# Three half-size weight buffers, squares on ScalarE, and projection weights staged in the arena of a three-part transformer layer

## The chip, the cores and the metric

The kernel runs on 8 cores of one Trainium2 chip. Each core takes 2 of the 16 sequences and works alone: no core talks to another. The metric is the device time in microseconds (us) of the slowest core.

TensorE (PE) multiplies, VectorE (DVE) and ScalarE (ACT) do the elementwise work and empty PSUM, GpSimd (POOL) and SyncE (SP) only issue DMA transfers here. ACT issues DMA transfers as well, from its own queue of instructions.

## The reference, cut to what matters

```python
def layernorm(x): return (x - mean(x)) / sqrt(var(x) + 1e-5)

def ffn(x):                       # D = 1024, H = 4096, per sequence of 2048
    h = x @ W1.T + scale * (x @ m1.T) + b1      # m1, m2: rank-4 products of
    h = gelu(h)                                 # rows 1..16 of x itself
    return h @ W2.T + scale * (h @ m2.T) + b2

def attn(x):                      # 8 heads of 128, causal
    xn = x / l2norm(x) * sqrt(1024) * gamma
    q, k, v = split(xn @ w_qkv.T)
    return softmax(mask(q @ k.T * 128**-0.5)) @ v @ w_out.T

x = x + 0.5 * ffn(layernorm(x))
x = x + attn(layernorm(x))
x = x + 0.5 * ffn(layernorm(x))
```

## The kernel before, in words

Everything is kept transposed: features on the 128 partitions, tokens along the free dimension. `R` holds the residual of one sequence in f32 (8 feature chunks `cc` of 2048 tokens), `xn` its normalised bf16 copy, and `arena` (64 KB in each partition, tracked as 32 slots of 1024 columns) holds either the hidden layer of an FFN tile of 1024 tokens or, in attention, four regions of 8192 columns: K at `KT0` (slots 0 to 7), V at `V0` (8 to 15), Q at `QT0` (16 to 23) and the attention output at `OA0` (24 to 31), for 4 heads at a time.

The program is one list of operations, written by Python in the order of the source. Each goes to the queue of one engine and keeps its place there; the class `Buf` works out from writers and readers of each slot which semaphores it waits for. So an instruction that waits holds up all behind it on its engine, DMA issues on SP and ACT among them. DMAs of one `group` also wait for the one before them in the group.

At the start `emit_prep` turns the f32 weights into bf16 in DRAM (`w1s`, `w2s`, `wqs`, `wos`) by way of arena slots 0 to 15. Then, for each of the 2 sequences: FFN, attention, FFN.

- **FFN** (`ffn`): 2 token tiles `ti` of 1024. The first product (L728, with the rank-4 part L739 and the GELU on ACT, L746) runs over 32 hidden chunks `hc`. Weights come by `wslab("w1", g, ...)`: 512 KB with 2 chunks, in turn into `wb0` and `wb1`. For each `nh` (512 tokens), 32 small matmuls (L765) and their evictions (L774) come first, then the second product (L797) over all hidden chunks into 8 PSUM banks at once; `wslab("w2", g, ...)` brings 2 chunks a time. Bias (ACT, L818) and residual (DVE, L826) end it, and then a *hook* runs.
- **LayerNorm** (`ln_block`, 512 tokens): sums over features by matmul with a column of ones (L473), squares on DVE (L483) into two halves of `sqt`, their sums by matmul (L488), then a chain of short row operations on ACT and DVE (L498 to L528), two rows sent to DRAM and back as broadcasts `rep_a` and `rep_b` (four DMAs issued by ACT, one group), and 16 DVE operations that write `xn` (L546/L550, or L553/L558 with gamma). In the first FFN the hook of `ti` 0, `nh` 0 has two such blocks in a row and that of `ti` 1, `nh` 0 has three, that of `ti` 1, `nh` 1 one. In attention, `attn_hook` puts one after each of the four token blocks of the last output projection; the one at `qb` 2 comes behind `lora_prep(part=1)`, with eight DMAs `e1z<-t` on ACT.
- **Attention** (`attn`), for each half `hh` of the heads: Q, K, then V projections from xn. `wslab` brings each weight as two slabs of 512 KB, part 0 to `wb0` and part 1 to `wb1`; every accumulation reads both. Q and K are evicted by ACT (L930, L926), V by DVE (L958), from 2 PSUM banks. After each head of K, `mhat_head` works out a bound for the softmax: 8 rounds of DVE square (L854), PE sum (L860), DVE maximum (L866), then Sqrt on ACT, and one number through DRAM (`browN`, `negm`), issued by ACT. Then units of 512 queries of a head: scores (L975, L986), Exp on ACT (L996), row sums (L1009) and P·V (L1019), and last the output projection (L1094, residual L1107) with two slabs of `wos`.

The two-buffer rotation:

```python
def next_w():
    i = wrot[0] % 2
    wrot[0] += 1
    return (wb0, "wb0") if i == 0 else (wb1, "wb1")
```

Of the kernel before, what the change touches and what calls it, by code (L numbers as in the profile page):

```python
# [251 lines left out]
def build(n_sub=3):  # L252
# [28 lines left out]
    with ctx:  # L281
# [146 lines left out]
        def wslab(kind, arg, wt, wbname, part=0):  # L428
            if kind == "w1":
                gate = prep_done["w1"][arg // 4]  # L430
            elif kind == "w2":
                gate = prep_done["w2"][arg // 4]
            elif kind in ("wq", "wk", "wv"):
                gate = prep_done["wq"][2 * part + 1]
            else:
                gate = prep_done["wo"][arg]
            deps = B(wbname).deps_write() + [gate]
            if kind == "w1":
                src = w1s[:, arg * 256:(arg + 1) * 256].rearrange("(cc p) h -> p cc h", p=128)
                dst = wt[:, :].rearrange("p (cc h) -> p cc h", cc=CC)  # L440
            elif kind == "w2":
                src = w2s[arg * 256:(arg + 1) * 256, :].rearrange("(hh p) o -> p hh o", p=128)
                dst = wt[:, :].rearrange("p (hh o) -> p hh o", hh=2)
            elif kind in ("wq", "wk", "wv"):
                f0 = {"wq": 0, "wk": 1, "wv": 2}[kind] * DM + arg * 512
                src = wqs[part * 512:(part + 1) * 512, f0:f0 + 512].rearrange(
                    "(cc p) f -> p cc f", p=128)
                dst = wt[:, :].rearrange("p (cc f) -> p cc f", cc=4)
            elif kind == "wo":
                r0 = arg * 512 + part * 256  # L450
                src = wos[r0:r0 + 256, :].rearrange("(fc p) c -> p fc c", p=128)
                dst = wt[:, :].rearrange("p (fc c) -> p fc c", fc=2)
# [794 lines left out]
```

How the kernel before makes its waits and increments, by code:

```python
            def run(engine_obj):  # L128
                hiwater = {}
                for op in oplist:
                    waits = {}
                    for d, m in op.deps:
                        if elided(e, d):
                            continue
                        s, v = d.sem, d.val
                        if m:
                            mo = margin_tok(d, op)
                            if mo is not None and mo.dma_group is None:
                                s, v = mo.tok.sem, mo.tok.val
                        assert s is not None, (e, op.tag, d.eng, d.idx)
                        if hiwater.get(s, 0) >= v:
                            continue
                        if waits.get(s, 0) < v:
                            waits[s] = v
                    for s, v in waits.items():
                        engine_obj.wait_ge(get_sem(s), v)
                        hiwater[s] = v
                        stats["waits"] += 1
                    ins = op.fn(engine_obj)
                    if op.needs_inc:
                        amt = 16 if op.dma_group is not None else 1
                        ins.then_inc(get_sem(op.tok.sem), amt)
                        stats["incs"] += 1
```

## Time and profile before

| | us |
|---|---|
| median of the 2 timed runs | 5114.68 (4993.43 and 5235.94) |
| the profiled execution, own time | 5005.92 |
| its span on the slowest core (core 1) | 5003.9 |
| spans of the 8 cores | 4958.5 to 5003.9 |
| PE busy | 3785.2 (76%) |
| ACT busy | 1165.2 (23%) |
| DVE busy | 868.2 (17%) |
| DMA traffic | 335.24 MB, mean 67 GB/s |

The span runs from the first to the last instruction; 2.0 us of the time lie around it. PE is busy for three quarters of the span, and what it waits for in the rest decides what a change is worth. A busy matmul of 128x512 is listed with a mean of 385 ns, but successive ones overlap: in a dense stretch one starts every 0.22 us. The granted clock of TensorE was 0.873 of full speed over the span of this core.

### The profile page before, as it was taken

To read this page: it belongs to the slowest core of one execution; us is meant where nothing else is said; L and a number is where in the kernel's file an instruction comes from. 1 tells how busy PE (TensorE), PEld (TensorE's weight loads), DVE (VectorE), ACT (ScalarE), POOL (GpSimd) and SP (SyncE) were. 2 spreads that over 40 slices of the span, in tenths; PEclk is the share of its full clock that TensorE was granted. 3 is DMA by queue.
4 is the path that set the end of the run, shared out by engine and by line. 5 is a ranking of instruction groups with operands and counts; after the bars stand their busy time and mean duration, and the time that the engine had idled before them with its cause. 6 is when DMAs were issued, how large, how long until landed. Compare 5 with 4: busy or idle time off the path is not lost.

```text
span 5003.9 us, 42288 instructions; the slowest of 8 cores (4958.5 to 5003.9 us)
## 1 busy us (share of the span) xinstructions
PE 3785.2 (76%) x14576; PEld 1307.5 (26%) x14576; DVE 868.2 (17%) x1403; ACT 1165.2 (23%) x1819; POOL 63.7 (1%) x114
## 2 busy tenths in 40 slices
PE   2068699676886865978969869957688686597997
PEld 0023133122222211323323313312222221133333
DVE  2000300523023034001010030052302303400000
ACT  0012121111631621311212212111163162131211
POOL 0000000000000000000000000000000000000000
PEclk7579799788997987989989979978799798798997
DMA  9952122120000000234233213212000000023323
GB/s 193 204 126 68 51 89 88 47 63 19 24 26 19 22 15 26 59 102 126 69 105 118 68 51 89 89 47 63 19 22 28 19 22 15 26 59 102 102 86 112
DMA packets 275837, 335.24 MB, mean 67 GB/s; under 512 B 20080, under 2 KB 163824, under 8 KB 275632
## 3 DMA queue, kind: packets, MB, share of 16 engines
q1 hardware_dynamic: 232688, 251.98, 16.6%
q0 software_dynamic: 18144, 50.34, 5.0%
q10 hardware_dynamic: 24800, 30.23, 2.1%
q8 instruction: 124, 2.03, 0.2%
q14 instruction: 81, 0.66, 0.0%
HBM read 315.16 MB, written 42.47 MB: 71 GB/s over the span
## 4 chain that ended last, share of the span: by engine, by line
PE 59%; DMA 20%; DVE 8%; ACT 6%; issue 6%; ACTq 1%; DVEq 0%; another core or an unknown queue 0%; SPq 0%; POOL 0%; POOLq 0%
PE ps L728 19%; PE ps L797 12%; DMA wb<-w2s 7%; PE ps L911 5%; PE ps L739 3%; PE ps L1009 3%; PE ps L1019 3%; PE ps L944 2%; PE ps L1094 2%; PE ps L765 2%; PE ps L986 2%; PE ps L473 2%; DMA arena<-w2T 2%; DMA rep_a<-browL 1%; ACT pb L996 1%
## 5 line engine op out<-in xcount | busy, mean ns | idle before, releaser
L728 PE MATMUL ps<-xn,wb 128*128 128x512 bf16 x4096 | 987.7, 385 | 105.6 <-DMA wb<-w1s 89.8
L797 PE MATMUL ps<-arena,wb 128*128 128x512 bf16 x4096 | 931.3, 385 | 66.9 <-DMA wb<-w2s 62.0
L797 PEld LDWEIGHTS ps<-arena,wb 128*128 128x128 bf16 x4096 | 392.7, 99 | 604.5 <-issue 212.3
L728 PEld LDWEIGHTS ps<-xn,wb 128*128 128x128 bf16 x4096 | 361.6, 98 | 598.1 <-issue 242.3
L746 ACT ACTIVATE arena<-ps,b1c 128x512 bf16<-128x512 f32 x512 | 351.3, 687 | 715.0 <-PE ps L739 698.8
L826 DVE SCALAR_TENSOR_TENSOR R<-f32t,R 128x512 f32<-128x512 f32 x128 | 88.6, 692 | 2462.8 <-ACT f32t L818 2462.8
L996 ACT ACTIVATE pb<-ps,negm 128x512 bf16<-128x512 f32 x640 | 419.3, 686 | 231.8 <-PE ps L986 135.1
L818 ACT ACTIVATE f32t<-ps,b2c 128x512 f32<-128x512 f32 x128 | 88.0, 687 | 1088.1 <-PE ps L811 987.9
L911 PE MATMUL ps<-xn,wb 128*128 128x512 bf16 x1024 | 273.3, 431 | 53.6 <-DMA wb<-wqs 22.3
L1009 PE MATMUL ps<-pb,onesc 128*1 128x512 bf16 x640 | 247.6, 387 | 80.3 <-ACT pb L996 80.3
L1019 PE MATMUL ps<-pb,arena 128*128 128x512 bf16 x640 | 255.6, 399 | 11.8 <-DVE arena L1047 11.8
L488 PE MATMUL ps<-sqt,onesc 128*1 128x512 bf16 x192 | 92.0, 494 | 227.0 <-DVE sqt L483 225.9
L986 PE MATMUL ps<-arena 128*128 128x512 bf16 x640 | 244.4, 391 | 17.7 <-ACT pb L996 17.7
L1094 PE MATMUL ps<-arena,wb 128*128 128x512 bf16 x512 | 137.5, 433 | 158.8 <-DVE R L1107 131.3
L473 PE MATMUL ps<-R,onesf 128*1 128x512 f32 x384 | 189.2, 646 | 46.7 <-DMA R<-xT 34.6
L739 PE MATMUL ps<-t,e1z 4*128 4x512 bf16 x512 | 198.6, 388 | 0.0
L860 PE MATMUL ps<-sqt,onesc 128*1 128x512 bf16 x128 | 65.5, 511 | 151.0 <-DVE sqt L854 151.0
L1047 DVE TENSOR_TENSOR arena<-ps,f32t 128x512 bf16<-128x512 f32 x64 | 44.2, 691 | 714.0 <-DMA f32t<-browF 305.9
L691 PE MATMUL ps<-xn,o1c 128*4 128x512 bf16 x160 | 63.7, 549 | 136.6 <-ACT t L700 58.6
L911 PEld LDWEIGHTS ps<-xn,wb 128*128 128x128 bf16 x1024 | 108.0, 108 | 218.2 <-issue 131.1
L866 DVE TENSOR_REDUCE nrm<-ps 1x1 f32<-1x512 f32 x128 | 86.9, 679 | 324.0 <-PE ps L860 324.0
L483 DVE TENSOR_TENSOR sqt<-R 128x512 bf16<-128x512 f32 x192 | 124.2, 687 | 106.3 <-PE ps L488 103.3
(81 smaller groups left out, 1810.2 us busy)
## 6 DMA issues: line engine op xcount, KB each, us to landing
wb<-w2s SPq DMA_DIRECT2D x256, 512.0 KB, 3.5
wb<-w1s SPq DMA_DIRECT2D x128, 512.0 KB, 4.0
f32t<-browF ACTq DMA_DIRECT2D x64, 256.0 KB
outT<-R POOLq DMA_DIRECT2D x64, 256.0 KB, 3.5
wb<-wqs SPq DMA_DIRECT2D x24, 512.0 KB, 4.0
arena<-w1T POOLq DMA_DIRECT2D x4, 2048.0 KB, 30.2
w1s<-arena SPq DMA_DIRECT2D x4, 2048.0 KB, 13.9
arena<-w2T POOLq DMA_DIRECT2D x4, 2048.0 KB, 39.0
```

Of the source, the lines that this page charges most:

```text
L473: t_sa = p.emit("pe", lambda e, cc=cc, n0=n0: e.matmul(ps[6][0:1, :], onesf[:, :], rsl(cc, n0), start=(cc == 0), stop=(cc == CC - 1)), dep ...
L483: t_sq = p.emit("dve", lambda e, cc=cc, n0=n0, pr=pr: e.tensor_mul(sqt[:, pr * 512:(pr + 1) * 512], rsl(cc, n0), rsl(cc, n0)), deps=B("R") ...
L728: t_mm = p.emit("pe", lambda e, cc=cc, hcl=hcl, n0=n0, wt=wt, bank=bank: e.matmul(bank[:, :], wt[:, cc * 256 + hcl * 128: cc * 256 + (hcl ...
L739: t_c1 = p.emit("pe", lambda e, hc=hc, nh=nh, bank=bank: e.matmul(bank[:, :], e1z[:, hc * 128:(hc + 1) * 128], t1[:, nh * 512:(nh + 1) * 5 ...
L746: t_g = p.emit("act", lambda e, hc=hc, nh=nh, bank=bank: e.activation(h_act(hc, nh), bank[:, :], AF.Gelu, bias=b1c[:, hc:hc + 1]), deps=[t ...
L797: t_mm = p.emit("pe", lambda e, oc=oc, hcl=hcl, hc=hc, nh=nh, wt=wt, bank=bank: e.matmul(bank[:, :], wt[:, hcl * 1024 + oc * 128: hcl * 10 ...
L911: t_mm = p.emit("pe", lambda e, cc=cc, ccl=ccl, h=h, nb=nb, wt=wt, bank=bank: e.matmul(bank[:, :], wt[:, ccl * 512 + h * 128: ccl * 512 + ...
L986: t_s = p.emit("pe", lambda e, kcol=kcol, qcol=qcol, bank=bank, diag=diag: e.matmul(bank[:, :], arena[:, kcol:kcol + 128], arena[:, qcol:q ...
L996: t_e = p.emit("act", lambda e, pslot=pslot, h=h, bank=bank: e.activation(pb[:, pslot * 512:(pslot + 1) * 512], bank[:, :], AF.Exp, bias=n ...
L1009: t_rs = p.emit("pe", lambda e, pslot=pslot, first=first, last=last, rsb=rsb: e.matmul(rsb[0:1, :], onesc[:, :], pb[:, pslot * 512:(pslot ...
L1019: t_pv = p.emit("pe", lambda e, vcol=vcol, pslot=pslot, first=first, last=last, ob=ob: e.matmul(ob[:, :], arena[:, vcol:vcol + 128], pb[:, ...
L1094: t_mm = p.emit("pe", lambda e, fc=fc, fcl=fcl, oc=oc, ocol=ocol, wt=wt, bank=bank: e.matmul(bank[:, :], wt[:, fcl * 1024 + oc * 128: fcl ...
```

## The change

1. Weight buffers: `wb0`, `wb1` of 2048 columns become `wb0`, `wb1`, `wb2` of 1024, in rotation. A slab holds one hidden chunk, 256 KB. So there are 32 slabs where there were 16. A `w1` slab was 1024 runs of 512 B (256 columns of 8 rows for each partition); now it is 1024 runs of 256 B. A `w2` slab was 256 runs of 2 KB and is 128.
2. `ln_block`: the squares are made by `activation(Square)` on ACT in place of `tensor_mul` on DVE.
3. Attention: V is projected first, then Q, then K. Each weight comes as one DMA of 1 MB into the arena: V's into the first half of the Q region, Q's and K's into the output region; the output projection's into the first half of the K region. `wb` isn't used there.

```diff
-        wb0 = sb("wb0", [128, 2048], BF16)
-        wb1 = sb("wb1", [128, 2048], BF16)
+        wb0 = sb("wb0", [128, 1024], BF16)
+        wb1 = sb("wb1", [128, 1024], BF16)
+        wb2 = sb("wb2", [128, 1024], BF16)
...
             if kind == "w1":
-                src = w1s[:, arg * 256:(arg + 1) * 256].rearrange("(cc p) h -> p cc h", p=128)
+                src = w1s[:, arg * 128:(arg + 1) * 128].rearrange("(cc p) h -> p cc h", p=128)
...
         def next_w():
-            i = wrot[0] % 2
+            i = wrot[0] % 3
             wrot[0] += 1
...
-                    t_sq = p.emit("dve", lambda e, cc=cc, n0=n0, pr=pr: e.tensor_mul(
-                        sqt[:, pr * 512:(pr + 1) * 512], rsl(cc, n0), rsl(cc, n0)),
+                    t_sq = p.emit("act", lambda e, cc=cc, n0=n0, pr=pr: e.activation(
+                        sqt[:, pr * 512:(pr + 1) * 512], rsl(cc, n0), AF.Square),
...
-                for g in range(16):
+                for g in range(32):
                     wt, wbn = next_w()
                     t_w = wslab("w1", g, wt, wbn)
...
-                for kind, reg0, scale_ev in (("wq", QT0, SCALE_ATTN), ("wk", KT0, None), ("wv", V0, None)):
-                    t_w0 = wslab(kind, hh, wb0, "wb0", part=0)
-                    t_w1 = wslab(kind, hh, wb1, "wb1", part=1)
...
+                def qkv_slab(kind, hh, col0):
+                    gate = prep_done["wq"][1]
+                    f0 = {"wq": 0, "wk": 1, "wv": 2}[kind] * DM + hh * 512
+                    src = wqs[:, f0:f0 + 512].rearrange("(cc p) f -> p cc f", p=128)
+                    dst = arena[:, col0:col0 + 4096].rearrange("p (cc f) -> p cc f", cc=CC)
+                    sl = aslot(col0, 4096)
+                    t = p.dma("sp", dst, src, deps=B("arena").deps_write(sl) + [gate],
+                              group="wA", tag=f"{kind}{hh}")
...
+                t_wv, wv_sl = qkv_slab("wv", hh, QT0)
+                for tt in range(16):
...
+                t_wq, wq_sl = qkv_slab("wq", hh, OA0)
+                t_wk, wk_sl = qkv_slab("wk", hh, OA0 + 4096)
...
-                t_wo0 = wslab("wo", hh, wb0, "wb0", part=0)
-                t_wo1 = wslab("wo", hh, wb1, "wb1", part=1)
+                src = wos[hh * 512:(hh + 1) * 512, :].rearrange("(fc p) c -> p fc c", p=128)
+                wo_sl = aslot(KT0, 4096)
+                dst = arena[:, KT0:KT0 + 4096].rearrange("p (fc c) -> p fc c", fc=4)
```

The first place where this moves instructions is DVE between two gamma-fused LayerNorm blocks of the first FFN's second tile. Before, the last write of `xn` of one block is followed by the next block's squares:

```order
L553 SCALAR_TENSOR_TENSOR f32t<-R,gamc,rep_a 128x512
L558 SCALAR_TENSOR_TENSOR xn<-rep_b,gamc,f32t 128x512
L483 TENSOR_TENSOR sqt<-R 128x512 x8
L506 TENSOR_TENSOR srow_c<-srow_a 1x512
L510 TENSOR_TENSOR srow_b<-srow_b,srow_c 1x512
L515 TENSOR_SCALAR srow_b<-srow_b 1x512
```

Now ACT has the squares, behind the two broadcast issues of the block before and ahead of its own short rows (L496 and L500 are L498 and L502 of before):

```order
L70 DMA rep_a<-browL 128x512
L70 DMA rep_b<-browL 128x512
L481 ACTIVATE sqt<-R 128x512 x8
L496 ACTIVATE srow_a<-ps 1x512
L500 ACTIVATE srow_b<-ps 1x512
L516 ACTIVATE srow_b<-srow_b 1x512
```

On DVE the block's first short row (L504, before L506) therefore stands right behind the last write of `xn`; on PE this place is unchanged.

The second place is PE from the last LayerNorm block of the first FFN to the first scores. Before, Q and the first head of K (160 matmuls), three more heads of K, then V, and the scores:

```order
L488 MATMUL ps<-sqt,onesc 1x512 x8
L911 MATMUL ps<-xn,wb 128x512 x160
L860 MATMUL ps<-sqt,onesc 1x512 x8
...
L911 MATMUL ps<-xn,wb 128x512 x32
L860 MATMUL ps<-sqt,onesc 1x512 x8
L944 MATMUL ps<-wb,xn 128x512 x128
L975 MATMUL ps<-maskm,ident 128x512
```

Now V comes first, and the bound of the last head is followed at once by the scores:

```order
L486 MATMUL ps<-sqt,onesc 1x512 x8
L913 MATMUL ps<-arena,xn 128x512 x128
L943 MATMUL ps<-xn,arena 128x512 x160
L858 MATMUL ps<-sqt,onesc 1x512 x8
...
L943 MATMUL ps<-xn,arena 128x512 x32
L858 MATMUL ps<-sqt,onesc 1x512 x8
L981 MATMUL ps<-maskm,ident 128x512
L992 MATMUL ps<-arena 128x512
```

V's 128 matmuls moved from between the last bound and the scores to the front, where the block of LayerNorm before them is still being written by DVE.

## Rows read from the trace of the kernel before

**Rows 1.** Groups by line (busy us, mean ns; idle before and its releasers).

```profile
L728 PE MATMUL ps<-xn,wb 128*128 128x512 bf16 x4096 | 987.7, 385 | 105.6 <-DMA wb<-w1s 89.8 <-ACT f32t L818 10.5 <-ACT arena L746 5.3
L797 PE MATMUL ps<-arena,wb 128*128 128x512 bf16 x4096 | 931.3, 385 | 66.9 <-DMA wb<-w2s 62.0 <-ACT u L774 3.1
...
L911 PE MATMUL ps<-xn,wb 128*128 128x512 bf16 x1024 | 273.3, 431 | 53.6 <-DMA wb<-wqs 22.3 <-DVE xn L558 16.1 <-ACT arena L930 12.6
...
L488 PE MATMUL ps<-sqt,onesc 128*1 128x512 bf16 x192 | 92.0, 494 | 227.0 <-DVE sqt L483 225.9
...
L518 ACT ACT_TABLE_LOAD x6 | 7.7, 1283 | 8.7 <-DVE srow_b L515 8.7
```

**Rows 2.** Waits: who waited for whom, us in total, times, longest us.

```profile
PE ps L797 <- DMA wb<-w2s: 62.0, 107, 2.5
```

**Rows 3.** Timeline of a second product: start us, us, engine, line, what, [idle before].

```profile
2155.42 7.08 PE L797 MATMUL ps<-arena,wb 128*128 128x512 bf16 x32
...
2159.13 3.81 SPq L70 DMA_DIRECT2D wb<-w2s  x2
...
2163.24 1.02 PE L797 MATMUL ps<-arena,wb 128*128 128x512 bf16 x4 [0.73 <-DMA wb<-w2s]
```

**Rows 4.** Windows: stretch, PE, PEld, DVE, ACT, POOL busy, PEclk, DMA share, GB/s.

```profile
470.00:520.00 50.00, 47.70 (x215) 20.12 (x214) 0.00 (x0) 0.00 (x0) 0.00 (x0) 1.00 0.42 137
690.00:810.00 120.00, 120.00 (x504) 44.12 (x503) 0.00 (x0) 38.31 (x57) 0.00 (x0) 1.00 0.21 62
```

**Rows 5.** DMA queue issued by ACT: packets, MB, share of 16 engines.

```profile
q10 hardware_dynamic: 24800, 30.23, 2.1%
```

**Rows 6.** Timeline of ACT's queue, the two broadcasts of a LayerNorm block.

```profile
1833.33 0.35 ACTq L70 DMA_DIRECT2D rep_a<-browL  x1
1836.42 0.35 ACTq L70 DMA_DIRECT2D rep_b<-browL  x1
```

**Rows 7.** Timeline of the hook with three LayerNorm blocks, first sequence.

```profile
917.34 0.35 ACTq L70 DMA_DIRECT2D rep_b<-browL  x1
...
932.58 0.75 DVE L558 SCALAR_TENSOR_TENSOR xn<-rep_b,gamc,f32t 128x512 bf16<-128x512 f32 x1
933.25 1.28 DVE L483 TENSOR_TENSOR sqt<-R 128x512 bf16<-128x512 f32 x2
...
940.82 0.68 DVE L510 TENSOR_TENSOR srow_b<-srow_b,srow_c 1x512 f32<-1x512 f32 x1 [0.99 <-ACT srow_b L502]
...
972.81 0.68 DVE L510 TENSOR_TENSOR srow_b<-srow_b,srow_c 1x512 f32<-1x512 f32 x1 [0.99 <-ACT srow_b L502]
...
982.57 7.93 PE L797 MATMUL ps<-arena,wb 128*128 128x512 bf16 x28 [2.13 <-ACT u L774]
```

**Rows 8.** Timeline of PE at the switch from Q to K.

```profile
1117.20 8.35 PE L911 MATMUL ps<-xn,wb 128*128 128x512 bf16 x32 [3.05 <-DMA wb<-wqs]
```

**Rows 9.** Timeline of the start of attention, PE and DVE.

```profile
1064.62 3.63 PE L911 MATMUL ps<-xn,wb 128*128 128x512 bf16 x16
...
1089.38 0.75 DVE L558 SCALAR_TENSOR_TENSOR xn<-rep_b,gamc,f32t 128x512 bf16<-128x512 f32 x1
...
1090.27 23.88 PE L911 MATMUL ps<-xn,wb 128*128 128x512 bf16 x97 [1.12 <-DVE xn L558]
```

**Rows 10.** Timeline from the last softmax bound of a half to its first exponentials.

```profile
1205.83 29.14 PE L944 MATMUL ps<-wb,xn 128*128 128x512 bf16 x128
...
1209.56 0.33 ACTq L70 DMA_DIRECT2D negm<-browN  x1
...
1235.48 1.28 ACT L996 ACT_TABLE_LOAD   x1 [27.48 <-PE ps L986]
...
1237.61 0.38 PE L1009 MATMUL ps<-pb,onesc 128*1 128x512 bf16 x1 [0.60 <-ACT pb L996]
```

**Rows 11.** Timeline of ACT in the attention hook at qb 2.

```profile
1920.65 5.64 ACTq L70 DMA_DIRECT2D e1z<-t  x4
...
1927.97 0.59 ACT L502 ACTIVATE srow_b<-ps 1x512 f32<-1x512 f32 x1 [0.99 <-PE ps L488]
```

More of the change, by code:

```diff
@@ L433, in wslab @@
+                dst = wt[:, :].rearrange("p (hh o) -> p hh o", hh=1)
             elif kind in ("wq", "wk", "wv"):
-                gate = prep_done["wq"][2 * part + 1]
+                gate = prep_done["wq"][part // 2]
+                f0 = {"wq": 0, "wk": 1, "wv": 2}[kind] * DM + arg * 512
+                src = wqs[part * 256:(part + 1) * 256, f0:f0 + 512].rearrange(
+                    "(cc p) f -> p cc f", p=128)
+                dst = wt[:, :].rearrange("p (cc f) -> p cc f", cc=2)
             else:
@@ L436, in wslab @@
                 gate = prep_done["wo"][arg]
+                r0 = arg * 512 + part * 128
+                src = wos[r0:r0 + 128, :].rearrange("(fc p) c -> p fc c", p=128)
+                dst = wt[:, :].rearrange("p (fc c) -> p fc c", fc=1)
             deps = B(wbname).deps_write() + [gate]
-            if kind == "w1":
-                src = w1s[:, arg * 256:(arg + 1) * 256].rearrange("(cc p) h -> p cc h", p=128)
[L440 to L452, printed above, removed]
@@ L788, in ffn @@
                     B("u4").wrote(t_uin)
-                    for g in range(16):
+                    for g in range(32):
                         wt, wbn = next_w()
@@ L793, in ffn @@
                             bank, bn = ps[oc], f"ps{oc}"
[L794 to L798 removed]
+                            for hcl in range(1):
+                                hc = g
+                                first = (hc == 0)
+                                t_mm = p.emit("pe", lambda e, oc=oc, hc=hc, nh=nh, wt=wt, bank=bank: e.matmul(
+                                    bank[:, :], wt[:, oc * 128:(oc + 1) * 128],
                                     h_act(hc, nh), start=(hc == 0), stop=False),
@@ new lines, in attn @@
+                t_wv, wv_sl = qkv_slab("wv", hh, QT0)
+                for tt in range(16):
+                    bank, bn = ps[tt % 2], f"ps{tt % 2}"
+                    last = None
+                    for cc in range(CC):
+                        t_mm = p.emit("pe", lambda e, cc=cc, tt=tt, bank=bank: e.matmul(
+                            bank[:, :], xn[:, cc * S + tt * 128: cc * S + (tt + 1) * 128],
+                            arena[:, QT0 + cc * 512: QT0 + (cc + 1) * 512],
+                            start=(cc == 0), stop=(cc == CC - 1)),
+                            deps=[t_wv] + B("xn").deps_read(rslot(cc, tt * 128)) +
+                                 (B(bn).deps_write() if cc == 0 else []), tag="wvmm")
+                        B("arena").read(t_mm, wv_sl)
+                        B("xn").read(t_mm, rslot(cc, tt * 128))
+                        if cc == 0:
+                            B(bn).wrote(t_mm)
+                        else:
+                            B(bn).accum(t_mm)
+                        last = t_mm
+                    col0 = V0 + tt * 512
+                    slots = aslot(col0, 512)
+                    t_ev = p.emit("dve", lambda e, col0=col0, bank=bank: e.tensor_copy(
+                        arena[:, col0:col0 + 512], bank[:, :]),
+                        deps=[last] + B("arena").deps_write(slots), tag="wvev")
+                    B(bn).read(t_ev)
+                    B("arena").wrote(t_ev, slots)
@@ L940, in attn @@
+                t_wq, wq_sl = qkv_slab("wq", hh, OA0)
+                t_wk, wk_sl = qkv_slab("wk", hh, OA0 + 4096)
+                for kind, wcol, wtok, wsl, reg0, scale_ev in (
+                        ("wq", OA0, t_wq, wq_sl, QT0, SCALE_ATTN),
+                        ("wk", OA0 + 4096, t_wk, wk_sl, KT0, None)):
+                    for h in range(HPH):
+                        for nb in range(4):
+                            bank, bn = ps[nb % 2], f"ps{nb % 2}"
                             last = None
@@ L951, in attn @@
+                                B("arena").read(t_mm, wsl)
+                                B("xn").read(t_mm, rslot(cc, nb * 512))
                                 if cc == 0:
```

106 lines of the change are left out of this document (36 added, 70 removed).

## The prediction

> **What bounds the kernel now.** I read the groups by line first, to see on what PE waits. PE is busy 3785.2 of 5003.9 us, so 1219 us are idle, and neither DVE nor ACT is busy for a quarter of it. The groups show three idle times that the change touches [rows 1]: 62.0 us before the second product L797, released by `wb<-w2s`; 22.3 us before the Q and K products L911, released by `wb<-wqs`; and 225.9 us before the sums of squares L488, released by the DVE squares. They show too where there is nothing to win: L728 waits on its weights once, 89.8 us at the start, behind the conversion of the weights, which the change leaves alone.
>
> Next the waits: the 62.0 us are 107 waits, none over 2.5 [rows 2], so a small shortfall that repeats. The timeline shows why [rows 3]. PE does 32 matmuls, two slabs, in 7.08 us; the slab issued at 2159.13, when the first buffer came free, releases PE at 2163.24, 4.11 us later, while the other buffer lasts about 3.6. So each pair of slabs costs some 0.5 to 0.7 us.
>
> Last, the timelines of the hooks. In them the chain is DVE's: it writes xn of one LayerNorm block until 933.3, only then squares the next one, and the variance row comes at 940.82 [rows 7].
>
> **The second product.** Three buffers of half the size leave the same cover: a buffer is refilled during two slabs of 8 matmuls, which is again 3.6 us. What changes is how long a slab takes. A w2 slab is now 128 rows of 2 KB, which is what the broadcast `rep_a` moves; issued at 1833.33 it had landed by 1836.42, 3.09 us later [rows 6]. With the 0.1 us in which SP sees the buffer free this is 3.2, less than 3.6: the wait goes. I keep 8 of the 62.0 us for stragglers and take -54. Bounds: -62, and if a half slab took the 4.11 us of a whole one, (4.11 - 3.63) x 512 slabs / 3 = 82 in place of 62, so +20. The row of the same shape is the nearest, so I stay near the lower end.
>
> **The first product.** The runs shrink from 512 to 256 B, and their number stays, 1024 for each slab, so it doubles in all. What a run costs now: in the window 690 to 810, 62 GB/s x 120 us are 14,500 runs of 512 B, and 0.21 x 16 engines x 120 us = 403 us, 27.7 ns each [rows 4]. The same from the window 470 to 520 gives 100 ns for 2 KB. Runs below 512 B are in ACT's queue: of its 24,800 packets 14,336 are rows of 2 KB (64 + 48 broadcasts of 128); at 100 ns they take 1439 of its 2.1% x 16 x 5003.9 = 1681 us and leave 23 ns for each of the 10,464 small ones [rows 5]. So a run of 256 B lies between 23 and 28 ns, at most 68, the mean over that queue. At 28 a slab keeps an engine busy for 64 x 28 ns = 1.8 us, and PE needs 18 matmuls x 120 us / 504 = 4.29 us for it [rows 4]. I take 0. The cover that would have to go is 4.29 us for 64 runs, 67 ns each.
>
> The Trainium skill speaks against this edit ("DMA: Bandwidth & Descriptors", Specifications): transfers reach line rate only from 512 B up, below that the engine reads, modifies and writes. No price is given there; if it meant twice the time of a 512 B run, 55 ns, the slab would take 3.5 us and would still be hidden, at a DMA share of 0.8. The trace shows no sign of it in the small packets of ACT's queue, but no row has runs of exactly this size.
>
> **Projection weights.** Q, K and V weights now go to regions that are free long before they are read: V's slots (16 to 19) during the last second product or after head 1's scores, Q's and K's during V. The wait of 22.3 us goes [rows 1]. There are three such switches in a sequence (Q to K twice, output projection to Q once). After one of them 32 matmuls took 8.35 us [rows 8] against 7.08 in a dense stretch [rows 3], so PE started slowly; 1.3 us x 6 are 8 us more. I take -30, bounds -22 and -32. The output weights were never waited for, so the fourth DMA is worth 0.
>
> **LayerNorm blocks that follow one another.** ACT issues `rep_b` of block 1 at 917.34 and is then free; its eight squares, 0.7 to 0.77 us each with PE's sums between, would be done by 924, well before DVE ends block 1 at 933.3 [rows 7]. DVE then goes straight to the short rows, and the variance row stands at 933.3 + 0.6 = 933.9 in place of 940.82: 6.9 us sooner. So again for the third block. It is this chain that ends the stall, not the squares alone: PE gets past block 3's sums much sooner, does its 32 small matmuls, and then waits for ACT to empty them, which is queued behind block 3's own broadcasts. That point, 982.57, moves by the chain's 2 x 6.9 and not by the 22 us by which PE's wait on squares shrinks. The hook of `ti` 0 has one such pair. Three pairs in each of two sequences: 6 x 6.9 = -41. The first block of each hook starts its squares half a DVE operation sooner, 8 blocks x 0.5 = -4. In attention's last projection the residual of the next block waits for DVE's writes of xn, and the squares wait for that residual on either engine: 0. Sum -45, bounds -41 (pairs only) and -60 (were the third block's earlier start all gain).
>
> ACT holds the squares at 0.69 us as its other 128x512 operations, and no table is loaded for them, which is my choice: a load takes 1.283 us, and 24 blocks would add 31 us at one each, 62 at two [rows 1]. The Trainium skill says that cheap functions are in every table set ("ScalarE: Activation LUTs", Table sets: the hidden batching unit), though its list doesn't name Square; by that rule the term is 0. The trace of before has no Square at all.
>
> **What the change adds.** (a) V is evicted by DVE, and V now comes first. In each sequence's first half DVE is writing xn until 1089.38 + 0.75 = 1090.1 [rows 9], so PE stops after two banks, 16 matmuls, near 1068 and goes on at 1090.8 with 112 + 128 to do. Before, at 1090.27, it had 97 + 128 left: 15 x 0.22 + 0.6 = +4 us, twice, +8. (b) The last head's bound was hidden by V. Its PE part ends at 1205.9, and ACT is free when `negm` is issued, 1209.56 + 0.33; behind that wait the table load 1.28 and the first Exp 0.69, 1211.9, so PE is without work for 6.0 us; before, the same point lay 2.7 us after V's end (1234.9 to 1237.61) [rows 10]. +3.3 x 4 = +13, bounds 0 and +24. (c) At `qb` 2 the squares stand on ACT behind eight DMAs `e1z<-t`, which last until 1926.3; the second sum came in at 1927.97 [rows 11]. Now eight squares of 0.61 to 0.69 come between, +5 x 2 = +10, bounds 0 and +12.
>
> **The sum.** -54 - 30 - 45 + 8 + 13 + 10 = -98. Against the profiled execution's own time, 5005.92 (its span and 2.0 around it), 4908 us. The median of the two runs shown, 5114.68, lies 109 above that execution, since one of the two took 5235.94; the other, 4993.43, agrees with it. The forecast is for executions like those two. It is 2.0% below, and 2% is about what a measurement of this kernel can tell, so this lies on the line.
>
> **The rivals.**
> - *The half slab takes nearly as long as the whole.* The waits of the second product stay at about 62 to 82. For it: 512 KB of w2 land in 4.11 us and 512 B runs of the same volume no slower, so much of a transfer is fixed. Against: 3.09 for the same shape [rows 6]. Time: 4908 + 54 to 74, about 4975. Chance 0.15.
> - *First product becomes DMA-bound: slower than before.* Place: every slab of L728, 256 of them. It decides from 67 ns for a run of 256 B, and outweighs the gains from 64 x p - 4.29 = 98 / 256 = 0.38 us on, p = 73 ns. At 80 ns: 0.83 x 256 = 212, 5120 us. For it: the halved runs, 8 cores at once. Against: 23 to 28 ns, and even the queue's mean of 68 is at the edge only. Chance 0.09.
> - *Table loads for Square.* +31 to +62 where half of them lie on the chain: about 4940 to 4970. Chance 0.08.
> - *More is gained than the waits.* PE restarts slowly after each of the long stalls in the hooks and projections, as in rows 8; if shorter stalls save this too, some 24 times 1.3 us, 4877. For it: mean granted clock 0.873. Against: the stalls of the hooks stay over 10 us. Chance 0.18.
> - *The change doesn't do what it says,* the chain behind DVE and ACT absorbing LayerNorm's part (-45 gone): 4953. Chance 0.08.
>
> The forecast has the remaining 0.42. Faster by over 2% (below 4906): half of the forecast's own 0.42 and most of the gain rival's 0.18 and a few of the others' tails, 0.43. Slower by over 2%: the DMA-bound case from 80 ns on, 0.06. Within 2%: 0.51. The range takes in all but the DMA-bound case and the far ends of the others; on the high side it adds the mishap of two small losses together: 4840 to 5030.
>
> **What would show it.** In the profile after: `PE ps L797`'s successor with under 15 us of waits on w2s and a landing below 3.6; no wait on w1s but the one at the start, and a DMA share near 0.4 in its windows, twice the 0.21 of before because the packets double (0.8 if a small run costs twice as much, 1.0 if the rival holds); no wqs waits; variance rows 26 us apart in the three-block hook where they were 32; PE idle for 6 us after each half's last bound, and for 22 after the first 16 V matmuls; table loads still near 22 in all. Wrong would be: w1s waits in numbers, or w2s waits as many as before.

## The result and the profile after

| | before | after |
|---|---|---|
| median of all timed runs | 4998.61 us (10 runs) | 4895.52 us (11 runs) |
| median of the 7 that count on each side | 4993.43 us | 4894.10 us |
| ratio, with its 95% interval | | 0.9798 [0.9786, 0.9809] |
| the profiled execution, own time | 5005.92 us | 4899.44 us |
| spans of the 8 cores | 4958.5 to 5003.9 us | 4865.5 to 4897.9 us |
| mean span of the 8 cores | 4983.9 us | 4878.8 us |

The change makes the kernel 2.0% faster, on the line between "same" and "faster" as forecast. In some executions four of the cores, or all eight, ran at a lower clock and took longer; the ratios and every median from here on leave them out (e8 has no other), and a trace that was taken in one (e1, e6, e8) is read only as far as is said there.

The groups by line of the kernel after, on its slowest core, beside [rows 1]:

```profile
L726 PE MATMUL ps<-xn,wb 128*128 128x512 bf16 x4096 | 986.8, 384 | 124.5 <-DMA wb<-w1s 108.4 <-ACT f32t L816 10.8 <-ACT arena L744 5.3
L795 PE MATMUL ps<-arena,wb 128*128 128x512 bf16 x4096 | 894.4, 380 | 32.2 <-ACT u L772 22.0 <-DMA wb<-w2s 9.6
L943 PE MATMUL ps<-xn,arena 128*128 128x512 bf16 x1024 | 246.3, 405 | 2.3 <-ACT arena L958 2.3
L913 PE MATMUL ps<-arena,xn 128*128 128x512 bf16 x512 | 116.7, 391 | 46.5 <-DVE arena L928 46.5
L486 PE MATMUL ps<-sqt,onesc 128*1 128x512 bf16 x192 | 93.8, 509 | 125.1 <-ACT sqt L481 118.0
L481 ACT ACTIVATE sqt<-R 128x512 bf16<-128x512 f32 x192 | 112.3, 623 | 228.2 <-PE ps L486 89.3 <-DVE R L1115 62.3 <-DMA rep_a<-browL 61.1
L516 ACT ACT_TABLE_LOAD x6 | 7.7, 1283 | 8.7 <-DVE srow_b L513 8.7
```

Four things are to be seen. The second product, now L795, waits 9.6 us for `w2s` where it waited 62.0, but also 22.0 us for ACT's `u`, and its *busy* time fell too, 931.3 to 894.4 on the slowest cores. The first product has one wait on `w1s`, as before:

```profile
PE ps L726 <- DMA wb<-w1s: 108.4, 1, 108.4
PE ps L795 <- ACT u L772: 22.0, 2, 11.0
PE ps L795 <- DMA wb<-w2s: 9.6, 13, 1.6
```

That one is the start (first product at 298.4 us before and 300.5 after, mean of the cores). The projections wait on no weights; V waits 46.5 us on its DVE evictions. And the sums of squares wait 118.0 us where they waited 225.9: 108 us of idle time less, in a kernel that became 105 us faster by all its edits together. Table loads are 22 in both, the group of six unchanged.

To see where the time went I cut each core's PE timeline at the same points in both kernels and took the mean over the 8 cores:

| stretch | before | after | difference | forecast |
|---|---|---|---|---|
| 16 second products | 984.0 | 925.4 | -58.6 | |
| hooks of the FFNs with LayerNorm | | | -66.2 | |
| the same two, ACT's wait for `u` (3.4 to 22.4) moved from the first to the second | | | -77.6; -47.2 | -54; -45 |
| projections Q, K, V, 4 halves | 649.3 | 623.3 | -26.0 | |
| output projection to the next half's Q or V | | | -7.5 | with the line above -22 |
| scores to the last P·V, 4 halves | 724.6 | 768.5 | +43.9 | +13 |
| attention hooks, 2 | 381.9 | 393.6 | +11.7 | +10 |
| start | 298.4 | 300.5 | +2.1 | 0 |
| 8 first products | 1127.1 | 1122.4 | -4.7 | 0 |
| whole | 4983.9 | 4878.8 | -105 | -98 |

The rows add up to -105, as the whole does. The 4.7 us of the first products are no gain of the change: they lie in the very first tile, which took 146.4 us in this execution of the kernel before, 139.5 in the kernel after, and 139.6 in e2 and e3 with the slabs of before.

So the total hides errors that nearly cancel: 24 us more gained in the buffers and 11.5 more in the projections than forecast, and 31 more lost in the scores. The scores are the surprise: they were not edited. This is the first half on one and the same core, a window from the first score to the last P·V (columns as in [rows 4]), before and then after:

```profile
1235.00:1416.00 181.00, 152.96 (x543) 38.28 (x541) 11.06 (x16) 122.78 (x191) 0.00 (x0) 0.98 0.09 28
```

```profile
1195.00:1392.00 197.00, 165.38 (x545) 39.28 (x544) 11.63 (x20) 123.30 (x193) 0.00 (x0) 0.91 0.11 31
```

The same instructions, the same 123 us of ACT; the column PEclk falls from 0.98 to 0.91 and the window is 16 us longer. Over the four halves, mean of the cores, the granted clock was 0.99, 0.964, 0.99, 0.984 before and 0.923, 0.945, 0.926, 0.944 after, that is less time at the upper of its two levels, 2.4 GHz. The halves don't lose alike: the two first ones went from 179.4 to 194.4 us, the two second ones from 184.6 and 181.1 to 189.8 and 189.7. On core 1 the second half of the first sequence didn't change at all, 188 us at 0.95 before and after:

```profile
1610.00:1798.00 188.00, 159.62 (x546) 38.75 (x544) 11.06 (x16) 122.78 (x191) 0.00 (x0) 0.95 0.09 27
```

```profile
1572.00:1760.00 188.00, 156.89 (x544) 38.83 (x543) 11.63 (x20) 123.11 (x192) 0.00 (x0) 0.95 0.12 32
```

Nor is it an even slowdown. The first 15 us of each half of the kernel after, and the rest (same core, first half and then second half):

```profile
1195.00:1210.00 15.00, 10.32 (x27) 2.31 (x26) 1.26 (x5) 7.14 (x12) 0.00 (x0) 0.78 0.01 1
1210.00:1392.00 182.00, 155.05 (x518) 36.98 (x518) 10.37 (x15) 116.16 (x183) 0.00 (x0) 0.92 0.12 34
1572.00:1587.00 15.00, 10.93 (x27) 2.32 (x26) 1.26 (x5) 6.50 (x10) 0.00 (x0) 0.60 0.01 1
1587.00:1760.00 173.00, 145.97 (x517) 36.50 (x517) 10.37 (x15) 116.61 (x182) 0.00 (x0) 0.98 0.13 34
```

PE enters both halves partly at the lower level. In the first half it also falls back to it again and again later (0.92 over the rest; 8 of the 13 windows of 15 us in it show 0.89), in the second hardly (0.98).

### The profile page after: what moved, and what is told of

Read it like the earlier page. It is cut to its first block, busy times and chain, and to the rows that moved or that the text cites. A ratio compares the mean times of both kernels' runs of the same rounds, so it can differ in the third digit from the quotient of the medians.

```text
span 4897.9 us, 43897 instructions; the slowest of 8 cores (4865.5 to 4897.9 us)
## 1 busy us (share of the span) xinstructions
PE 3756.5 (77%) x14576; PEld 1311.6 (27%) x14576; DVE 747.6 (15%) x1211; ACT 1275.4 (26%) x2011; POOL 63.7 (1%) x114
## 4 chain that ended last, share of the span: by engine, by line
PE 65%; DMA 14%; DVE 7%; ACT 7%; issue 5%; ACTq 1%; DVEq 0%; another core or an unknown queue 0%; SPq 0%; POOL 0%; POOLq 0%
PE ps L726 19%; PE ps L795 17%; PE ps L943 5%; PE ps L737 3%; PE ps L1015 3%; PE ps L1025 3%; PE ps L1102 2%; PE ps L763 2%; PE ps L913 2%; PE ps L992 2%; DMA browF<-srow_a 2%; DMA arena<-w2T 2%; DMA rep_a<-browL 1%; ACT pb L1002 1%; ACT f32t L816 1%
## 5 line engine op out<-in xcount | busy, mean ns | idle before, releaser
L726 PE MATMUL ps<-xn,wb 128*128 128x512 bf16 x4096 | 986.8, 384 | 124.5 <-DMA wb<-w1s 108.4
L795 PE MATMUL ps<-arena,wb 128*128 128x512 bf16 x4096 | 894.4, 380 | 32.2 <-ACT u L772 22.0
L795 PEld LDWEIGHTS ps<-arena,wb 128*128 128x128 bf16 x4096 | 397.8, 98 | 527.9 <-issue 60.3
L726 PEld LDWEIGHTS ps<-xn,wb 128*128 128x128 bf16 x4096 | 361.4, 98 | 615.8 <-issue 259.5
L992 PE MATMUL ps<-arena 128*128 128x512 bf16 x640 | 255.1, 408 | 19.7 <-ACT pb L1002 19.7
L1102 PE MATMUL ps<-arena 128*128 128x512 bf16 x512 | 143.7, 448 | 155.2 <-DVE R L1115 127.5
L943 PE MATMUL ps<-xn,arena 128*128 128x512 bf16 x1024 | 246.3, 405 | 2.3 <-ACT arena L958 2.3
L486 PE MATMUL ps<-sqt,onesc 128*1 128x512 bf16 x192 | 93.8, 509 | 125.1 <-ACT sqt L481 118.0
L481 ACT ACTIVATE sqt<-R 128x512 bf16<-128x512 f32 x192 | 112.3, 623 | 228.2 <-PE ps L486 89.3
L913 PE MATMUL ps<-arena,xn 128*128 128x512 bf16 x512 | 116.7, 391 | 46.5 <-DVE arena L928 46.5
L1015 PEld LDWEIGHTS ps<-pb,onesc 128*1 128x1 bf16 x640 | 50.6, 79 | 374.5 <-issue 374.5
```

The costliest lines, as they stand in the source:

```text
L726: t_mm = p.emit("pe", lambda e, cc=cc, n0=n0, wt=wt, bank=bank: e.matmul(bank[:, :], wt[:, cc * 128:(cc + 1) * 128], xsl(cc, n0), start=(c ...
L795: t_mm = p.emit("pe", lambda e, oc=oc, hc=hc, nh=nh, wt=wt, bank=bank: e.matmul(bank[:, :], wt[:, oc * 128:(oc + 1) * 128], h_act(hc, nh), ...
L913: t_mm = p.emit("pe", lambda e, cc=cc, tt=tt, bank=bank: e.matmul(bank[:, :], xn[:, cc * S + tt * 128: cc * S + (tt + 1) * 128], arena[:, ...
L943: t_mm = p.emit("pe", lambda e, cc=cc, h=h, nb=nb, wcol=wcol, bank=bank: e.matmul(bank[:, :], arena[:, wcol + cc * 512 + h * 128: wcol + c ...
L992: t_s = p.emit("pe", lambda e, kcol=kcol, qcol=qcol, bank=bank, diag=diag: e.matmul(bank[:, :], arena[:, kcol:kcol + 128], arena[:, qcol:q ...
L1015: t_rs = p.emit("pe", lambda e, pslot=pslot, first=first, last=last, rsb=rsb: e.matmul(rsb[0:1, :], onesc[:, :], pb[:, pslot * 512:(pslot ...
```

## The experiments

Ten kernels ran, e1 to e10. The kernel before ran beside each of them, the kernel after did not; differences to the kernel after are taken from its 4894.10 us, those to the kernel before from its 4993.43.

### One part at a time: which edit gives what

e1 is the kernel after with its squares back on DVE, so buffers and attention alone:

```diff
-                    t_sq = p.emit("act", lambda e, cc=cc, n0=n0, pr=pr: e.activation(
-                        sqt[:, pr * 512:(pr + 1) * 512], rsl(cc, n0), AF.Square),
+                    t_sq = p.emit("dve", lambda e, cc=cc, n0=n0, pr=pr: e.tensor_mul(
+                        sqt[:, pr * 512:(pr + 1) * 512], rsl(cc, n0), rsl(cc, n0)),
```

> The changed kernel with the squares back on DVE, so attention part plus three half-size buffers. Beside the kernel with the attention part alone it gives the price of the buffers. Theory A (a stall costs more than the idle time listed for it, because the last matmul before it runs out its full 380 ns in place of the 216 ns pitch): the buffers are worth about 95 us, the sum of the 16 second products falls from 998 to about 900 us. Rival B (my forecast: only the listed 62 us can go): about 54 us. Time: A 4905, B 4945. Without the squares on ACT there is no ACT-bound wait of 12 us at the start of two of the second products.

Measured 4920.98 us (4920.15 and 4921.80), ratio 0.9839 [0.9697, 0.9981]. Of its trace only the waits are read, on core 1:

```profile
PE ps L795 <- DMA wb<-w2s: 8.5, 11, 3.0
PE ps L795 <- ACT u L772: 4.4, 2, 2.7
```

The waits on `w2s` are down to 8.5 us without the squares too, and of the 22 us of waits on ACT only 4.4 are there: the rest belongs to the squares.

e2 is the kernel before with only that edit made (Square on ACT).

> The kernel before with the squares on ACT alone. Chain theory: three pairs of blocks in each of two sequences save 6.9 us each (-41), singles -4, the block behind the e1z DMAs loses 5 to 6 in each sequence (+10 to +12): -33, about 4965. Rival (the squares on ACT only move the wait): no change, 4998. Variance rows in the three-block hook 26 us apart in place of 32, table loads still 22 to 23.

Measured 4960.13 us in the one execution that counts, 33 below the kernel before, as the chain theory said; one execution gives no interval. Its hooks agree with those of the kernel after to 0.2 us (first sequence, mean of the cores: the two-block hook 77.6 before and 70.2 and 70.0 now; the three-block hook 84.8 and 61.0 in both), and so do its attention hooks (196.9 and 197.0, before 191.1 and 190.8). The squares' part is thus separate from the rest: -47.2 in the FFNs and +11.7 in attention, -35.5.

e3 is the kernel before with only part 3 of the change, attention's order and weights.

> The kernel before with the attention part alone (V, Q, K order, weights staged in the arena, V's evictions on DVE, two full-size buffers elsewhere). Theory A (the order V, Q, K takes away a dense run ahead of the scores, and their granted clock falls from 1.00 to about 0.91): projections gain about 35 us, the scores lose about 30, so about 4995, and the scores of a first half take 193 to 197 us where they took 181. Rival B (my forecast: -30, +8, +13 from waits alone): the scores lose 3.3 us each, about 4989, at a clock of 1.00.

Measured 5004.15 us, ratio 1.0017 [0.9977, 1.0057]. The attention part alone gives nothing. It saves the same on the projections (first halves 171.7 to 167.8, second 153.3 to 142.9) and loses it in the scores: 767.2 against 724.6, granted clock 0.934, 0.925, 0.963, 0.921. Theory A is near by its total (4995) and its sizes (-35 and +30 expected; -36, the switch to the next half with it, and +42 measured), though not by the place: the first halves took 191.5 and 188.2 us, under the 193 to 197 expected, and the second ones 193.4 and 193.9, more than in the kernel after. Its second product waits as before:

```profile
PE ps L797 <- DMA wb<-w2s: 68.7, 116, 2.8
```

From e3 to e1 is the buffers alone: 5004.2 to 4921.0, -83 (-79 between the fastest executions), which agrees with the -77.6 of the table and not with the -54 of the forecast, nor with the 95 that theory A gave.

**Where the other 24 us of the buffers were.** e2 and the kernel after have the same squares and the same waits on ACT, so their second products differ by the buffers alone: 999.3 and 925.4, 74 us. The listed waits on `w2s` fell by 51.3 (59.8 to 8.5, mean of the cores), as forecast; the busy time of L797 fell by 21.6 (914.6 to 893.0). A matmul followed closely by another counts its pitch, 216 ns (the 7.08 us of 32 in [rows 3] are 31 x 0.216 and one of 0.38), and the last before a stall counts its whole 0.38. Each of the 101 stalls that went (114 to 13, mean of the cores) therefore also took 0.16 us of "busy" with it, 16 us (an estimate); stalls shorter than that wouldn't be listed at all, which may be the other 5, but that is argued and not measured.

### The order of Q, K and V: why the scores became slower

e4 is the kernel after with Q, K and V in the old order and the weights still in the arena (Q's and K's in V's region, V's in the output region):

```diff
-                t_wv, wv_sl = qkv_slab("wv", hh, QT0)
-                for tt in range(16):
...
+                t_wq, wq_sl = qkv_slab("wq", hh, V0)
+                t_wk, wk_sl = qkv_slab("wk", hh, V0 + 4096)
+                do_qk("wq", V0, t_wq, wq_sl, QT0, SCALE_ATTN)
+                t_wv, wv_sl = qkv_slab("wv", hh, OA0)
+                do_qk("wk", V0 + 4096, t_wk, wk_sl, KT0, None)
+                do_v(range(16), OA0, t_wv, wv_sl, "dve")
```

> The changed kernel with the order Q, K, V again, all weights still staged in the arena (Q's and K's in the V region, V's in the output region). It takes away V's stall behind DVE and puts the dense V run back ahead of the scores. Clock theory: the scores of a first half take 181 to 183 us again at a granted clock of 1.00 for most of it (193 to 197 at about 0.91 in the changed kernel), and all four scores together give back about 30 us, the V stall another 8: 38 us below the changed kernel, 4858. Rival (only the uncovered tail of the last bound, 3.3 us four times, and the stall): 21 us, 4875, with the clock of the scores unchanged.

Median 4882.0 us, lowest 4870.75, ratio 0.973 [0.9644, 0.9816]: 12 below the kernel after by the medians, 21.5 by the mean span of the profiled executions. The scores are back to 737.5 from 768.5; in the first half core 1 is again at 0.98 and 181 us:

```profile
1197.00:1378.00 181.00, 153.37 (x545) 38.45 (x543) 11.07 (x16) 122.95 (x191) 0.00 (x0) 0.98 0.11 34
```

The projections cost 622.6, as in the kernel after (623.3): the weights in the arena are what gains, and the new order is what costs. V first puts the stop-and-go products of the last bound straight ahead of the scores; V last puts 128 dense matmuls there. So the order explains 31 of the 43.9 us that the scores lost, the uncovered hole of 3.3 us four times among them. The other 13 are there with V last too (737.5 against 724.6); most of that is in the second halves (187.6 and 187.3), and it stays open. The time misses the 4858 of the clock theory by 24: by those 13, and because the 8 us of V's stall didn't come. The first halves' projections gained 2.4 us each, the second ones lost 1.4 and 2.5, and the switch from output projection to the next half went from 37.1 to 40.4, twice.

e6 splits V in the first half: tiles 0 to 11 first, evicted by ACT, then Q and K, then tiles 12 to 15, so that 32 dense matmuls stand ahead of the scores; the second half goes Q, K, V.

```diff
+                    do_v(range(12), OA0 + 4096, t_wv, wv_sl, "act")
+                    do_qk("wq", KT0, t_wq, wq_sl, QT0, SCALE_ATTN)
+                    do_qk("wk", OA0, t_wk, wk_sl, KT0, None)
+                    do_v(range(12, 16), OA0 + 4096, t_wv, wv_sl, "dve")
```

> As e4, but in the first half of each sequence V's first 12 token tiles come first, with evictions on ACT, and its last 4 after K. It should keep what e4 gains on the tail of the bound and what e5 gained at the start: if both causes are real and separate, 4830 to 4845, the fastest of all. If 32 dense matmuls (7 us) ahead of the scores are too few for the clock, the scores of the first half stay near 190 us and the time lies near 4850.

Median 4855.29 us, lowest 4849.61, ratio 0.9676 [0.957, 0.9781]; the stages are read from e9 below, which has the same order. That is 39 below the kernel after, but short of the 4830 to 4845 expected and near the 4850 of the case in which 32 dense matmuls are too few.

### V's evictions

e5 is the kernel after with V evicted by ACT in each sequence's first half, where DVE is still writing xn:

```diff
+                    if hh == 0:
+                        t_ev = p.emit("act", lambda e, col0=col0, bank=bank: e.copy(
+                            arena[:, col0:col0 + 512], bank[:, :]),
```

> The changed kernel with V's evictions on ACT in the first half of each sequence. If the 23 us stall behind V's first two banks is DVE writing xn, PE goes on as soon as ACT has issued the second broadcast, about 16 us sooner, twice: -32, about 4863. Rival (V would wait for xn of the last token block anyway): V reaches that block only after 96 matmuls, 21 us, so at most 3 us of the gain are lost; if it waited sooner the gain would be under 10 us in all.

Median 4864.17 us, ratio 0.9726 [0.9645, 0.9807]; -30, and -32 was expected. The stall it removes, in the kernel after on core 3, and what is left of it in e5 on core 1:

```profile
1030.09 3.63 PE L913 MATMUL ps<-arena,xn 128*128 128x512 bf16 x16
...
1055.41 0.75 DVE L556 SCALAR_TENSOR_TENSOR xn<-rep_b,gamc,f32t 128x512 bf16<-128x512 f32 x1 [0.17 <-DVE f32t L551]
1056.91 18.28 PE L913 MATMUL ps<-arena,xn 128*128 128x512 bf16 x73 [23.20 <-DVE arena L928]
```

```profile
1022.54 3.63 PE L913 MATMUL ps<-arena,xn 128*128 128x512 bf16 x16
1033.32 0.13 PEld L913 LDWEIGHTS ps<-arena,xn 128*128 128x128 bf16 x2 [7.65 <-issue]
1033.35 16.96 PE L913 MATMUL ps<-arena,xn 128*128 128x512 bf16 x71 [7.18 <-ACT arena L929]
```

PE stops after 16 matmuls in both, for 23.2 and for 7.2 us; the first half's projections go from 168.5 to 152.2. The scores gain nothing (773.7 against 768.5), so a shorter stall at the head of the projections doesn't bring their clock back.

### The hook at qb 2

e7 is the kernel after with `ln_block` ahead of `lora_prep`, so that the squares stand before the eight DMAs `e1z<-t` on ACT:

```diff
                     elif qb == 2:
-                        lora_prep(part=1)
                         ln_block(NT, False)
+                        lora_prep(part=1)
```

> The changed kernel with ln_block(NT) ahead of lora_prep(part=1) in the attention hook at qb 2, so the squares on ACT don't stand behind the e1z DMAs. Theory: the 5 to 6 us by which the attention hooks grew in each sequence come back and some of lora_prep hides behind the LayerNorm chain: -12 to -30, about 4875. Rival (lora_prep's own PE and ACT steps now wait behind the broadcasts instead): 0, 4896.

Measured 4862.2 us (4857.27 to 4866.94), ratio 0.9696 [0.959, 0.9801]; -32, beyond the expected range by 2. The hooks take 181.2 each in place of 196.8. In the kernel after, ACT's timeline shows the squares behind the DMAs, and PE then waits 20.77 us for the residual that DVE does after its xn writes:

```profile
1889.63 5.62 ACTq L70 DMA_DIRECT2D e1z<-t  x4
...
1895.35 1.15 ACT L481 ACTIVATE sqt<-R 128x512 bf16<-128x512 f32 x2 [5.80 <-DMA e1z<-t]
...
1901.68 0.59 ACT L500 ACTIVATE srow_b<-ps 1x512 f32<-1x512 f32 x1 [0.35 <-PE ps L486]
...
1926.66 5.65 PE L1102 MATMUL ps<-arena 128*128 128x512 bf16 x13 [20.77 <-DVE R L1115]
```

In e7 the second sum leaves ACT at 1881.02, the DMAs follow behind the broadcasts, and PE restarts without that wait:

```profile
1881.02 0.59 ACT L500 ACTIVATE srow_b<-ps 1x512 f32<-1x512 f32 x1 [0.35 <-PE ps L486]
...
1898.87 5.62 ACTq L70 DMA_DIRECT2D e1z<-t  x4
...
1899.45 3.59 PE L1102 MATMUL ps<-arena 128*128 128x512 bf16 x8
...
1906.40 5.95 PE L1102 MATMUL ps<-arena 128*128 128x512 bf16 x19 [3.36 <-ACT t L620]
```

### How far w1 is from being bound by its transfers

e8 loads each w1 slab twice into the same buffer, doubling the small runs and nothing else:

```diff
+            if kind == "w1":
+                t = p.dma("sp", dst, src, deps=deps, group=grp, tag=f"{kind}{arg}.x")
+                B(wbname).wrote(t)
+                deps = B(wbname).deps_write() + [gate]
```

> The changed kernel with every w1 slab loaded twice, one after the other, before it is used. Runs of 256 B cost 18 ns in the changed kernel's window (0.28 x 16 x 110 us over 27,000 runs): two loads in series take about 2 x 3.0 us from issue, 6.1, under the 8.6 us of cover, so no wait on w1s beyond the start and a DMA share near 0.56; time within 10 us of the changed kernel. Rival (small runs near their limit with 8 cores at once): waits on w1s in numbers, over 100 us more.

It has no time that counts (4998, 5010 and 5127 us). The stage can be read on core 0, whose granted clock (0.874) is that of the kernel after. The window of the first product, in the kernel after (core 3) and in e8 (core 0):

```profile
680.00:790.00 110.00, 110.00 (x462) 40.52 (x461) 0.00 (x0) 36.15 (x53) 0.00 (x0) 1.00 0.28 63
```

```profile
690.00:790.00 100.00, 98.43 (x407) 36.39 (x415) 0.00 (x0) 31.62 (x46) 0.00 (x0) 1.00 0.56 120
```

In the kernel after 63 GB/s x 110 us are 27,070 runs of 256 B, and 0.28 x 16 x 110 = 493 us, 18.2 ns each, less than the 27.7 of a 512 B run [rows 4] though not half of it. In e8 the share doubles to 0.56 and PE is nearly always busy; its waits on w1s go from one to 30,

```profile
PE ps L730 <- DMA wb<-w1s: 128.4, 30, 105.8
```

of which 105.8 is the start, so 22.6 us are new, 0.09 for each of 256 slabs. As in the second product the stage lost more than is listed: the eight first products of core 0 took 1152.2 us against 1123.1, 29 us, which alone is more than the 10 expected for the whole kernel (mean of all cores +45, not all at that clock). The whole span of core 0 is only 10.5 longer, 4896.9 against 4886.4, since its scores took 23 less. Twice the runs are mostly hidden, not wholly; at the single load the cover is far from gone.

### The best version

e9 joins e6's order and e7's swap; e10 joins e4's order and e7's swap. No edit is new.

> The split V order and the swapped hook together. If the two gains add (scores and projections in one, 15.7 us in each of two attention hooks in the other), about 31 below the split order alone, 4815 to 4825, ratio near 0.962. If 32 dense matmuls ahead of the scores are enough for the clock, the scores of a first half take 180 to 183 us at 0.98; if not, near 190.

> The order Q, K, V with staged weights and the swapped hook. Gains add: 31 below the order Q, K, V alone (4871), 4840, ratio near 0.966; scores 737 us in all as in that kernel, attention hooks 181 each.

e9: median 4816.12 us (4806.95 to 4820.68), ratio 0.9623 [0.9596, 0.9649], 1.6% below the kernel after: the best. The gains add: against the kernel after the projections take 30 us less, the scores 33, the attention hooks 31, and the switch to the next half 6 more. Its scores are 183.3, 183.0, 184.8, 184.0, sum 735.1; in the first half of core 1:

```profile
1175.00:1359.00 184.00, 155.87 (x542) 38.42 (x541) 11.02 (x16) 122.46 (x191) 0.00 (x0) 0.96 0.12 34
```

With 32 dense matmuls ahead of the scores the first halves run at 0.973 and 0.960 (mean of the cores), between the 0.923 and 0.926 of none in the kernel after and the 0.985 and 0.977 of 128 in e4. The mean hides a scatter: in the second sequence three cores took 192 us at 0.92, as without any, and three 177.5 to 177.7 at 1.00. And the second halves of e9, where Q, K and V are those of e4 and e10, took 183.0 and 184.0 us at 0.98 and 0.975, where e4 took 187.6 and 187.3 and e10 188.0 and 185.2. So something besides the order decides 1 to 5 us a half; no run here shows what.

e10: 4834.43, 4846.42 and 4899.57 us, ratio 0.9738 [0.964, 0.9837], scores 736.1, hooks 181.1 and 180.6. The stages agree with what was expected, and the expected 4840 lies between its two lower times; with three times 65 us apart it says no more.

## Why the prediction was right, and where it was not

The forecast was 4908 us and 2.0% faster; 4895.5 and 2.0% were measured. The number is in part luck: two terms were too small by 24 and 11.5 us and one too small by 31 the other way. Most of the mechanisms were right. Term by term:

- **Second product, -54: mechanism right, size -78 (-74 to -83 by two pairs of kernels).** The three small buffers do what the working said: a half slab lands in 2.6 us (median of the DMA issues), below the 3.09 that it was given, and 9.6 of the 62.0 us stay where 8 were kept. The 4.11 us given for a whole slab was one that PE waited for; the median landing was 3.5, just under the cover of 3.6, so that 107 of 256 slabs came late. What failed is taking the listed idle time as the whole price of a stall. The bound of -62 was made the same way, and the measured value lies outside it.
- **First product, 0: right.** One wait, no sign of the bound case. The run of 256 B costs 18.2 ns, below the 23 that I gave as the lower end: that bound rested on a mean over other small transfers in ACT's queue [rows 5]. The share is 0.28 where I wrote near 0.4, for the same reason.
- **Projection weights -30 and V's evictions +8, together -22: measured -26 and -7.5.** The waits on `wqs` went as said, and PE stands 23.2 us behind the first 16 V matmuls (forecast 22). The size was off by 11.5 us, past the bound of -32 on the weights: the second halves' projections alone went from 153.3 and 152.2 to 142.9 and 143.2, and the switch from the output projection to the next half, which the forecast counted among its six, gave another 3.8 each time. The slow restarts that I priced at 1.3 us from a single one of them were larger; their clock is part of it (0.92 over 43 us of Q and K in the second half of the kernel before on core 1, 1.00 over 37 us of V's end, Q and K after). V's stall came out at some 5 us in all by e4 against the kernel after, not 8. And e5 shows that what it costs against no stall is 16 us a sequence: the +8 was meant against the kernel before, which had most of that stall at the same place.
- **LayerNorm blocks, -45: right, -47.2.** The chain between the blocks is what counts, not PE's idle time. The timeline of the three-block hook after, beside [rows 7]:

```profile
890.27 0.68 DVE L508 TENSOR_TENSOR srow_b<-srow_b,srow_c 1x512 f32<-1x512 f32 x1 [0.33 <-ACT srow_b L500]
...
900.06 0.35 ACTq L70 DMA_DIRECT2D rep_b<-browL  x1
...
900.46 1.15 ACT L481 ACTIVATE sqt<-R 128x512 bf16<-128x512 f32 x2 [6.27 <-DMA rep_a<-browL]
...
916.67 0.68 DVE L508 TENSOR_TENSOR srow_b<-srow_b,srow_c 1x512 f32<-1x512 f32 x1
...
931.70 8.92 PE L763 MATMUL ps<-arena,o2c 128*4 128x512 bf16 x32
...
942.23 0.68 DVE L508 TENSOR_TENSOR srow_b<-srow_b,srow_c 1x512 f32<-1x512 f32 x1
...
952.18 5.09 PE L795 MATMUL ps<-arena,wb 128*128 128x512 bf16 x14 [11.02 <-ACT u L772]
```

  The variance rows are 26.4 and 25.6 us apart where they were 32.0, the squares begin at 900.46, right behind `rep_b`, and PE, which is through the hook 24 us sooner, pays 11.0 of that back by waiting for ACT. Net 14 to 15 us for this hook; 2 x 6.9 was forecast.
- **No table load for Square: right.** 22 loads before and after. One of them stands at a Square, the first activation of the program, and costs nothing more, as it stood at L498 before:

```profile
L481 ACT ACT_TABLE_LOAD x1 | 1.3, 1283 | 35.2 <-DMA R<-xT 35.2
```

  The other 191 Squares, among stages with other functions, brought none. The Trainium skill says that cheap functions stand in every set ("ScalarE: Activation LUTs", Table sets: the hidden batching unit), though it doesn't list Square; these 191 agree with Square being one of them. The square took 0.62 us where 0.69 was assumed.
- **The last bound uncovered, +13: mis-sized, +44 measured.** The hole itself is as worked out, from the end of the bound's sums to the first row sum:

```profile
1198.36 0.58 PE L858 MATMUL ps<-sqt,onesc 128*1 128x512 bf16 x1 [1.33 <-DVE sqt L852]
...
1202.38 0.33 ACTq L70 DMA_DIRECT2D negm<-browN  x1
...
1202.79 1.28 ACT L1002 ACT_TABLE_LOAD   x1 [1.95 <-DMA browN<-nrm]
...
1204.92 0.45 PE L1015 MATMUL ps<-pb,onesc 128*1 128x512 bf16 x1 [3.30 <-ACT pb L1002]
```

  PE finishes the bound at 1198.94 and adds up its first row at 1204.92, 6.0 us as forecast. What failed is that the term stopped there. What lies behind that point ran at a lower granted clock, some 12 us more in each first half and 2 and 5 in the second ones, and its upper bound of +24 was for the hole only. The runs show that most of it follows the order of the projections: 767 to 774 with V first (e3, after, e5, e7), 725 to 738 with V last (before, e2, e4, e10), 735 with a quarter of V last in the first halves (e9). That the clock follows from the stop-and-go stretch ahead of the scores fits this, but isn't shown: a kernel that puts work of no use there, to separate it from the order, wasn't run, most of the low clock comes in spells well behind the start of a first half, and halves with the same order differ by up to 5 us (e9 against e4 and e10).
- **The squares at `qb` 2, +10: right, +11.7.** The price of the place was seen; that swapping two lines would take away 31 us in all, more than undoing the edit, was not looked for.

Of the rivals, "more is gained" was half right: of 35.5 us more, 24 were in the second product, which it didn't name, 11.5 in the projections, which it did, and none behind the hooks. "Half slab as slow" and "DMA-bound" fell with the landing of 2.6 us and the single wait on w1s. The Trainium skill's rule that only transfers of 512 B and more reach line rate ("DMA: Bandwidth & Descriptors", Specifications) holds here in that a byte costs more in short runs, 0.071 ns against 0.054; the price of a run did not double but fell by a third, and it was hidden.

## What to carry to other kernels

A repeated short stall costs more than the idle time listed for it: count the stalls, and compare the length of the stage with its instructions at full pace. When a block of dense matmuls is moved, look at what comes after its old place too; here the stage behind it lost 31 us, 13 of them the hole that was opened and the rest granted clock. And where a shift of work puts it behind waiting DMA issues on a queue, try the other order of the two before giving up either.

## What was unexpected of the hardware

- The scores of the first halves ran at a granted clock of 0.97 to 0.99 behind 128 dense matmuls (before, e2, e4, e10), 0.96 and 0.97 behind 32 (e9) and 0.92 to 0.96 straight behind the bound's sums (after, e3, e5, e7), each the mean of the cores over 179 to 197 us in which the clock falls to its lower level in spells.
- Reads of 256 B runs cost a DMA engine 18.2 ns each, against 27.7 for 512 B and 100 for 2 KB.
- Whole transfers, median from issue to landing in the kernel after; 512 KB of w2 had taken 3.5 us before:

```profile
wb<-w2s SPq DMA_DIRECT2D x512, 256.0 KB, 2.6
wb<-w1s SPq DMA_DIRECT2D x256, 256.0 KB, 3.0
...
arena<-wqs SPq DMA_DIRECT2D x12, 1024.0 KB, 5.1
```
